# A decoder layer on one core: the gate of every early gate/up product through tanh, and a new order of calls

## The reference

```python
# x: (8,128,128), ctx: (8,128,128), mask: (8,128,128)
q, k, v = heads(x)                    # 16 heads, 64 wide
w   = softmax(causal(q @ k.T) / 8)
x1  = layernorm(x + concat(w @ v) @ w_o.T)
qc, kc, vc = x1 @ Wq.T + bq, ctx @ Wk.T + bk, ctx @ Wv.T + bv   # 16 heads, 8 wide
wc  = softmax(where(mask == 0, -1e9, qc @ kc.T / sqrt(8)))
x2  = layernorm(x1 + concat(wc @ vc) @ Wo.T + bo)
logits = x2 @ router_w.T              # 8 experts; top two, with a jitter threshold
dense_w = sparsemixer(logits)         # (tokens, 8), two entries per token
y = sum over e of dense_w[:, e] * ((silu(x2 @ w_gate[e].T) * (x2 @ w_up[e].T)) @ w_down[e].T)
out = layernorm(x2 + y)
```

## Time and profile before

| | |
|---|---|
| time, median of 3 | 233.08 us (233.04 to 233.16) |
| the profiled execution, its own time | 233.06 us |
| its span, first to last instruction | 231.0 us |
| TensorE busy | 225.9 us (98%) |
| VectorE busy | 192.1 us (83%) |
| ScalarE busy | 164.9 us (71%) |
| GpSimd busy | 102.0 us (44%) |
| granted TensorE clock | 1.00 throughout |

### The profile page before, as it was taken

One profiled execution on the slowest core, in us unless ns is written; L12 is line 12 of the kernel. 1 busy time (PEld: TensorE's weight loads), 2 busy tenths in 40 slices (PEclk: granted clock), 3 DMA queues, 4 the chain that ended last, 5 costly groups with the idle time before them and its releaser, 6 DMA issues.

```text
span 231.0 us, 6982 instructions
## 1 busy us (share of the span) xinstructions
PE 225.9 (98%) x2274; PEld 205.9 (89%) x2274; DVE 192.1 (83%) x954; ACT 164.9 (71%) x552; POOL 102.0 (44%) x162
## 2 busy tenths in 40 slices
PE   8999999999999999999999999999999999999992
PEld 8999888997978988978978988789999999999992
DVE  3897798997889889989899879989898565766984
ACT  3768988898999979999989999697476333333001
POOL 4387738796396568922978351231200000100112
PEclk9999999999999999999999999999999999999999
DMA  6998000000000000000002200000000000000000
GB/s 189 362 363 314 10 0 0 4 3 1 3 1 3 0 6 3 0 3 1 1 4 64 121 3 3 3 0 4 0 3 0 1 3 0 4 23 0 26 23 24
DMA packets 7011, 9.10 MB, mean 39 GB/s; under 512 B 1088, under 2 KB 5824, under 8 KB 6592
## 3 DMA queue, kind: packets, MB, share of 16 engines
q1 hardware_dynamic: 4320, 7.09, 8.7%
q10 hardware_dynamic: 2656, 1.57, 2.3%
HBM read 8.14 MB, written 0.52 MB: 37 GB/s over the span
## 4 chain that ended last, share of the span: by engine, by line
PE 96%; DVE 1%; issue 1%; POOL 1%; ACT 0%; POOLq 0%; ACTq 0%; DVEq 0%
PE bank L1545 13%; PE bank L1443 11%; PE bank L1445 10%; PE bank L1444 10%; PE bank L2043 9%; PE bank L1527 7%; PE bank L1554 7%; PE bank L1595 6%; PE bank L1563 4%; PE bank L1538 3%; PE bank L1611 2%; PE bank L1482 2%; PE bank L1483 2%; PE bank L1484 2%; PE bank L1570 2%; PE bank L2053 1%
## 5 line engine op out<-in xcount | busy, mean ns | idle before, releaser
L525 ACT ACTIVATE probs_s<-masked_s,nmax_s 128x128 f32<-128x128 f32 x128 | 49.8, 396 | 3.6 <-DVE nmax_s L839 2.1
L311 POOL TENSOR_TENSOR probs_s<-probs_s,rec_sum_s 128x512 f32<-128x512 f32 x32 | 33.1, 1040 | 35.0 <-DVE rec_sum_s L846 34.8
L586 ACT ACTIVATE silu<-bank 128x256 f32<-128x256 f32 x54 | 20.1, 384 | 30.3 <-PE bank L1445 28.4
L528 ACT ACTIVATE probs_c<-masked_c,nmax_c 128x128 f32<-128x128 f32 x128 | 40.3, 396 | 1.6 <-DVE nmax_c L839 1.4
L1443 PE MATMUL bank<-ctx_hi,gu_hi 128*128 128x256 f32 x128 | 38.7, 302 | 0.0
L1444 PE MATMUL bank<-ctx_lo,gu_hi 128*128 128x256 f32 x128 | 35.7, 279 | 0.0
L1445 PE MATMUL bank<-ctx_hi,gu_lo 128*128 128x256 f32 x128 | 35.7, 279 | 0.0
L839 DVE CUSTOM_DVE_ANT_0 masked_c<-bank,mask_add 128x128 f32<-128x128 f32 x128 | 29.0, 286 | 4.6 <-PE bank L1538 3.9
L839 DVE CUSTOM_DVE_ANT_0 masked_s<-bank,causal 128x128 f32<-128x128 f32 x128 | 29.2, 285 | 1.2 <-PE bank L1527 1.0
L503 POOL TENSOR_TENSOR mv<-mv,minus_half 128x1 f32<-128x1 f32 x7 | 3.8, 556 | 55.2 <-DVE mv L1388 55.2
L1443 PEld LDWEIGHTS bank<-ctx_hi,gu_hi 128*128 128x128 f32 x128 | 24.3, 190 | 0.7 <-DVE qk_a L969 0.3
(11 more groups left out here) (180 smaller groups left out, 591.4 us busy)
## 6 DMA issues: line engine op xcount, KB each, us to landing
raw<-in_gateT SPq DMA_DIRECT2D x1, 1024.0 KB, 8.2
raw<-in_upT SPq DMA_DIRECT2D x1, 1024.0 KB, 12.1
down_sb<-in_down SPq DMA_DIRECT2D x1, 1024.0 KB, 5.2
raw<-in_wvT SPq DMA_DIRECT2D x1, 512.0 KB, 5.6
ctxT_all<-in_ctxT SPq DMA_DIRECT2D x1, 512.0 KB, 6.9
masked_c<-in_mask ACTq DMA_DIRECT2D x1, 512.0 KB, 11.9
wo_sb<-in_woT SPq DMA_DIRECT2D x1, 512.0 KB, 6.1
x_tok<-in_x ACTq DMA_DIRECT2D x1, 512.0 KB, 11.2
```

The source lines that it names most:

```text
L311: pool.tensor_tensor(probs_s[:, g % 2], probs_s[:, g % 2], spread(rec_sum_s[:, 4 * g:4 * g + 4], 2, S), ALU.mult).then_inc(normed[g], 1)
L525: last = act.activation(probs_s[:, g % 2, i, :], masked_s[:, g % 2, i, :], ACT.Exp, scale=-1.0, bias=nmax_s[:, h:h + 1], accum_out=rsum_s[ ...
L528: last = act.activation(probs_c[:, g % 2, i, :], masked_c[:, g % 2, i, :], ACT.Exp, scale=-1.0, bias=nmax_c[:, h:h + 1])
L586: act.activation(silu[:, i % NS, :], g, ACT.Silu).then_inc(silued, 1)
```

## The change

`NTANH` goes from 10 to 32: products 10 to 31 take tanh on ScalarE and two instructions on VectorE. `gate` and `hidden` themselves are as before. `FILL_BANK` is another list; its last eight entries, the banks of products 24 to 31, are the same. All four lists of calls are written anew: the same calls with the same work, some in other places, many with other banks, and the written waits of TensorE to match. The diff, cut to the constants, to GpSimd around `own_k(6)` and `own_k(7)`, to ScalarE's and VectorE's late parts, and to TensorE's list from `gate_up(7)` on:

```diff
-    NTANH = 10
+    NTANH = 32
...
-        FILL_BANK = [OC, OC, X0, OS, OC, T1, Y0, X0, OC, X1, Y0, OS, X1, Y0, OS, T0,
-                     T1, Y0, X0, T1, X1, Y1, OC, T0, X0, Y0, OS, OC, X1, Y1, T0, T1]
+        FILL_BANK = [OC, X0, X0, Y0, OC, T1, Y0, X0, T0, Y1, X0, OC, T0, Y1, X0, OS,
+                     OC, Y0, X0, OS, Y1, X1, T0, T1, X0, Y0, OS, OC, X1, Y1, T0, T1]
...
 # GpSimd
+            padded_v(6)
+            normalise(0, 7)
+            root(var2_done, pow2_done, mv2, 3)
+            normalise(1, 7)
             own_k(6)
-            normalise(3, 6)
-            add_out_bias(5)
-            normalise(2, 6)
-            padded_v(5)
-            root(var2_done, pow2_done, mv2, 3)
-            own_k(7)
-            split_x2(1)
-            normalise(0, 7)
-            normalise(1, 7)
             root(var1_done, pow1_done, mv1, 6)
             normalise(2, 7)
             normalise(3, 7)
-            padded_v(6)
+            root(var2_done, pow2_done, mv2, 4)
             split_x2(2)
             add_out_bias(6)
-            root(var2_done, pow2_done, mv2, 4)
             root(var1_done, pow1_done, mv1, 7)
+            own_k(7)
             split_x2(3)
...
 # ScalarE
             gate(6)
             gate(7)
-            evac_turned("c", 2, 7, T0)
-            evac_turned("c", 3, 7, T1)
+            evac_turned("c", 2, 7, T1)
+            evac_turned("c", 3, 7, X1)
             gate(8)
             gate(9)
-            evac_oc(7, Y1)
+            evac_oc(7, OC)
             gate(10)
...
 # VectorE
             hidden(8)
             hidden(9)
-            divide_c(7, T0)
+            divide_c(7, Y0)
             hidden(10)
-            evac_ccatT(7, T0)
+            evac_ccatT(7, Y0)
             hidden(11)
+            evac_logits(5, OS)
+            residual2(7, X1)
+            hidden(12)
             evac_x2T(6, T1)
-            residual2(7, T0)
-            hidden(12)
-            evac_logits(5, X0)
             hidden(13)
             normalise_x2(7)
             hidden(14)
-            evac_x2T(7, X0)
+            evac_x2T(7, T1)
             evac_logits(6, X1)
             hidden(15)
-            evac_logits(7, OS)
+            evac_logits(7, T1)
+            hidden(16)
             rank_0()
-            hidden(16)
+            hidden(17)
             rank_1()
+            hidden(18)
             rank_2()
-            hidden(17)
+            hidden(19)
             rank_3()
-            hidden(18)
+            hidden(20)
             rank_4()
-            hidden(19)
+            hidden(21)
             rank_5()
-            hidden(20)
-            hidden(21)
             hidden(22)
             rank_6()
             hidden(23)
...
 # TensorE, around products 10 to 31 (the new list; unchanged ones between them left out)
+            pe.wait_ge(hid_done, 8)
             gate_up(10)
+            turn_oc(7, Y0)
+            gate_up(11)
+            turn_ccat(7, Y0)
+            gate_up(12)
+            route(5, OS)
+            project_out_c(7, X1)
+            gate_up(13)
+            gate_up(14)
             turn_x2(6, T1)
+            pe.wait_ge(logit_evac, 6)
             gate_up(15)
+            gate_up(16)
             route(6, X1)
+            turn_x2(7, T1)
             gate_up(17)
+            route(7, T1)
             gate_up(18)
-            pe.wait_ge(hid_done, 17)
+            pe.wait_ge(hid_done, 16)
             gate_up(19)
...
             pe.wait_ge(hid_done, 19)
             gate_up(24)
             gate_up(25)
+            pe.wait_ge(hid_done, 20)
             gate_up(26)
-            pe.wait_ge(hid_done, 23)
             gate_up(27)
+            pe.wait_ge(hid_done, 22)
             gate_up(28)
             gate_up(29)
+            pe.wait_ge(hid_done, 23)
+            gate_up(30)
             pe.wait_ge(hid_done, 24)
-            gate_up(30)
             gate_up(31)
```

More of the change, by code:

```diff
@@ L394, in _ @@
             split_x(1)
-            round_ctx(0)
             split_x(2)
@@ L399, in _ @@
             normalise(1, 0)
-            round_ctx(1)
-            split_cwk()
-            scale_cwq()
+            round_ctx(0)
+            key_bias()
             normalise(2, 0)
             normalise(3, 0)
-            key_bias()
+            split_cwk()
+            round_ctx(1)
+            scale_cwq()
+            padded_v(0)
+            split_gu(0)
             normalise(1, 1)
             normalise(0, 1)
+            own_k(0)
             normalise(3, 1)
@@ L410, in _ @@
             normalise(2, 1)
-            own_k(0)
-            split_gu(0)
             normalise(0, 2)
-            normalise(1, 2)
+            padded_v(1)
             add_out_bias(0)
             root(var1_done, pow1_done, mv1, 1)
+            normalise(1, 2)
+            add_out_bias(1)
             split_gu(1)
-            add_out_bias(1)
-            padded_v(0)
             own_k(1)
-            split_gu(2)
             normalise(2, 2)
@@ L424, in _ @@
             own_k(2)
-            padded_v(1)
+            root(var1_done, pow1_done, mv1, 2)
+            padded_v(2)
             normalise(0, 3)
-            root(var1_done, pow1_done, mv1, 2)
-            add_out_bias(2)
-            padded_v(2)
             normalise(1, 3)
             own_k(3)
-            split_gu(3)
             normalise(2, 3)
             normalise(3, 3)
-            split_gu(4)
-            normalise(0, 4)
-            root(var2_done, pow2_done, mv2, 0)
-            normalise(1, 4)
-            root(var1_done, pow1_done, mv1, 3)
-            padded_v(3)
-            add_out_bias(3)
-            split_gu(5)
-            normalise(2, 4)
+            split_gu(2)
+            own_k(4)
+            normalise(0, 4)
+            add_out_bias(2)
+            root(var1_done, pow1_done, mv1, 3)
+            normalise(1, 4)
+            root(var2_done, pow2_done, mv2, 0)
+            normalise(2, 4)
+            add_out_bias(3)
+            split_gu(3)
+            split_gu(4)
             normalise(3, 4)
-            split_gu(6)
-            split_gu(7)
-            own_k(4)
+            own_k(5)
             normalise(0, 5)
@@ L1147, in _ @@
+            group_max("s", 3, 3, Y0)
+            residual1(2, X0)
+            reciprocal_s(1, 3)
+            divide_c(0, T0)
+            reciprocal_s(0, 3)
+            group_max("s", 2, 3, Y1)
+            normalise_x1(2)
+            evac_v(3, 1, X0)
+            evac_x1T(2, OS)
+            evac_v(3, 0, T0)
+            evac_qk(3, 3, OC)
+            evac_qc(2, OS)
+            lower_qc(2, OS)
+            evac_ccatT(0, Y1)
             evac_turned("s", 1, 3, Y0)
+            group_max("c", 0, 2, OC)
@@ L1290, in _ @@
             group_max("c", 3, 7, OS)
[L1291 removed]
+            divide_c(6, X1)
+            evac_logits(4, T0)
+            evac_x2T(5, OC)
+            evac_ccatT(6, X1)
             hidden(5)
[L1293 to L1296 removed]
+            residual2(6, Y1)
             hidden(6)
@@ new lines, in _ @@
+            turn("s", 1, 1, Y0)
+            pe.wait_ge(v_evac[0], 2)
+            turn("s", 0, 1, X1)
+            pe.wait_ge(maxed["s"][2], 2)
+            project_out_s(0, OC)
+            project_v(2, 0, T0)
+            pe.wait_ge(kc_lower, 1)
+            next_qk(1, 0, OS)
+            pe.wait_ge(kc_lower, 2)
+            score_s(2, 0, X0, T1)
+            mix_s(1, 0, Y0)
+            turn("s", 2, 1, X1)
+            turn_x1(0, OC)
+            pe.wait_ge(qk_evac[0], 2)
+            turn("s", 3, 1, OS)
@@ L1919, in _ @@
+            turn("c", 0, 5, Y1)
+            turn("s", 1, 7, X1)
+            turn("c", 1, 5, T0)
+            pe.wait_ge(hid_done, 1)
+            route(1, OC)
+            pe.wait_ge(turned_evac["s"][0], 8)
+            turn_oc(4, OS)
+            gate_up(1)
+            pe.wait_ge(turned_evac["c"][0], 6)
+            turn_x1(6, Y1)
+            mix_s(7, 0, OC)
+            project_qc(6, T1)
+            turn("c", 2, 5, OS)
             pe.wait_ge(turned_evac["c"][1], 6)
-            turn("c", 2, 5, X0)
```

879 lines of the change are left out of this document (420 added, 459 removed).

## The result

The changed kernel took 242.54 us (median of 4 runs, 241.85 to 243.34) against 233.12 us before on the same chip: ratio 1.0403, 95% interval 1.038 to 1.0426, 9.4 us slower. The forecast was 239.0 us, with a range up to 241.5; the result lies outside. The profiled execution took 241.85 us with a span of 239.8 us, 8.8 us more than before.

What follows compares the result with a forecast made beforehand. TensorE's stream was taken to bound the kernel, with VectorE's second parts putting it behind. Profiled span 231.0 + 5.9 = 236.9 us, table loads and order adding nothing, + 2.06 = 239.0 us; range 236.2 to 241.5.

Steps and rivals of the forecast that it cites:

- The bound: TensorE's stream, busy 225.9 of 231.0 us, sets the time; VectorE is nearly as full from 148 to 177.5 us.
- The second parts, +5.9 us: Products 10 to 31 get a second VectorE instruction; TensorE's down_product(0, 3) then starts 5.9 us late.
- 9.9 - 0.8: VectorE's queue up to product 31: 22 x 0.45 = 9.9 us added, 0.8 us of it absorbed by pauses.
- The lower price, 0.11 us each: If a tanh product's first VectorE part cost only its pipelined 0.34 us: 2.4 us less, +3.5 in all.
- rival 1: Table loads decide and VectorE swallows the second parts: 232.8 us, or 230.5 with both loads on the path; chance 0.05.
- The table loads: On ScalarE one load is left, ahead of product 32; the saving is only the 0.26 us wait already in the 0.8.
- the cover that was named: The remaining load, near 184 us, has 2 us of cover before hidden(32); without it the load would cost 1.3.
- I take 0 for the whole order, between -3.1 and +1.5: The new order of calls in 0 to 157 us costs nothing, with bounds of -3.1 and +1.5 us.
- change nothing in this sum: The moved routing steps, the same ones in the same late stretch, add nothing to VectorE's queue.
- rival 4: TensorE's clock falls as it idles in 171 to 187 us: 4.6 us, 2 hidden behind VectorE, about 241.8; chance 0.07.
- Rival 2: The new order closes TensorE's holes, all 3.1 us gone and VectorE earlier by the same: 235.9 us; chance 0.10.
- rival 3: The new order opens holes through own_k(6) and its like: 0.8 to 1.5 us more, about 240.3; chance 0.08.

Runs made afterwards that it cites:

- e3: The changed kernel with products 27, 30 and 31 multiplied 3, 2 and 4 times over, so TensorE works through its holes; 241.69 us.
- e4: The changed kernel with GpSimd's own_k(7) moved from behind the last root of the first layernorm to behind normalise(3, 7); 241.18 us.
- t2: The changed kernel (32 tanh products) with own_k(7), split_gu(0) and spread_mask() moved, and the routing calls earlier; 240.17 us.
- t3: The changed kernel (32 tanh products) with own_k(7), split_gu(0) and spread_mask() moved, and TensorE's holes filled with repeated multiplications; 240.10 us.
- h4: The kernel before with 32 tanh products and product 26 multiplied four times over; 239.47 us.
- h3: The kernel before with 24 tanh products and product 26 multiplied four times over; 238.71 us.
- e1: The changed kernel with NTANH back at 10, the new order alone; 237.09 us, ratio 1.0161.
- t1: The new order with ten tanh products, own_k(7), split_gu(0) and spread_mask() moved, and the routing calls earlier; 234.46 us.
- h1: The new order with ten tanh products, own_k(7) and split_gu(0) put back, spread_mask() in a VectorE pause; 235.17 us.

## Why the prediction was wrong

**The bound.** Right: TensorE's stream sets the time, and the change put VectorE ahead of it in 170 to 187 us. Two readings on the way were wrong and changed no term: VectorE is busy 10.40 + 9.57 = 20.0 us of 148 to 170, not 19.3, which adds the weight loads' 9.73 of the first stretch to VectorE's 9.57 of the second; and in the old list bank T0 of product 23 goes to `gate_up(30)`, which started at 174.09, 1.4 us behind it, and not to `gate_up(31)` 2.1 us behind.

**The second parts, +5.9 us.** Right in each term. 0.79 us per product (182.12 to 182.90); VectorE 27.2 us from `divide_c(7)` to the operation behind product 31, against 18.2, +9.0 where 9.9 - 0.8 was forecast; no pause; the block of products 24 to 31 6.3 us. At full clock the distance is 31.15 to 31.23 us in four traces of the new order (e3, e4, t2, t3), 5.9 to 6.0 more than the 25.25 before, and 31.35 in h4, the old order. The lower price, 0.11 us each, and rival 1 are refuted. That 24 tanh products cost 5.4 us of distance at full clock (h3, 30.63 us) and 32 only 5.9 fits the same account.

**The table loads.** Right: one is left,

```profile
185.76 1.28 ACT L586 ACT_TABLE_LOAD   x1 [0.39 <-DVE qk_a L966]
```

in the cover that was named, 2.2 us ahead of `hidden(32)`. Rival 1's mechanism gave nothing.

**"I take 0 for the whole order, between -3.1 and +1.5": this step failed.** The order alone costs 3.7 us (3.3 to 4.2 by its interval), more than twice the upper bound; within the changed kernel, whose last stretch doesn't pay the 0.6, it is 1.5 us in the profiled run, and 2.2 by the medians, as what is left: 242.54 less 233.12, 5.95 and 1.3. The bound was built from one call, `own_k(6)`, as the worst place, and that place did little: the root there waited for VectorE's `mv`, to 131.89 us. Of `own_k(7)` I wrote "with little to spare" and gave it no price. It cost 0.7 us in the new order and 1.35 in the old one, and not by being late: I had priced GpSimd's calls only by when they end, and not by what they hold while they run. The rows for that were in hand: two 1.04 us operations put directly behind the operation that releases a VectorE one. Two other places showed. The mask call ahead of `reciprocal_s(3, 0)` costs 0.8 to 1.1 us where the mask lands late, by the traces of e1 and e3; moving it brought the medians nothing clear. The routing calls behind two more products cost 0.4 us, with ten products only. I had priced both as free: of the routing I wrote that it would "change nothing in this sum", and the mask call I never named.

**The clock, rival 4 at 0.07.** It happened in all four runs of the changed kernel (mean clock 0.983 to 0.993), with the mechanism as described and a smaller price: in the profiled run 3.41 us at half clock, of which 1.3 reach the end (32.52 against 31.2), where 2.6 was forecast. That the lower level doubles a step is right by the changed kernel's own rows: `gate_up`'s matmuls start 0.21 us apart from 184.19 us on and 0.12 apart from 187.64 on. The 20 matmuls of the earlier trace rows could not show it: they are as slow as that, but the profile has the granted clock at 1.00 over them. The chance was too low. I had the idle third of 171 to 187 us in my own account of the changed kernel, and took the forecast's clock from a stretch in which TensorE never stopped.

Together, for the profiled run: 239.0 forecast, +1.3 for the clock, +1.5 for the order, 241.8, and it took 241.85. The median lies 0.7 us above that run; the mask's landing can do as much, but the other runs have no trace. Both errors have one sign, and each was a rival with a chance of its own; the range of 236.2 to 241.5 held either one alone, not the two together. Rival 2 (the new order closes holes) is refuted by the order alone; rival 3 was right in kind, at other places, and at 1.5 to 2.2 us where it had 0.8 to 1.5.

**What stays open.** t1 is still 1.3 us above the kernel before. In h1, which has the same start, TensorE shows no wait between 17.9 and 40.2 us and yet needs 22.3 us for the same calls that took 21.7. Which neighbours of calls make that I did not separate. h1's six runs still differ by 1 us with the mask out of the way; why, no trace shows, and `project_cv(0)` alone starts up to 0.8 us apart in the traces. Nor was the new order tried with its GpSimd calls moved from beside the other `normalise_x1` calls: the first of them took 1.21 us in the changed kernel, at 34.43, against 0.34 before, and two more took 0.76 and 0.94. Why the clock falls in one run of a kernel and not in the next stays open too.

## What to carry to other kernels

Where VectorE and GpSimd both work in SBUF, price a moved GpSimd operation by what VectorE has to do while it runs, and not only by its own start and end; the worst place is directly behind the small operation that VectorE waits for. If an added load puts a second engine ahead of TensorE, add the clock: TensorE's holes can cost again behind them, and more instructions put into the hole can make the kernel faster. Compare runs with the fall with runs that have it. And an order made anew is not free because it holds the same calls: each call that stands behind other work than before is a term of the sum. A call that waits for a transfer costs in some executions and not in others, so one trace can put down its price too high or miss it.

## What the runs showed of the hardware

- A VectorE operation of 128x128 floats from SBUF to SBUF took 0.35 us alone and 1.05 beside a GpSimd operation of 1.03 us that had begun 0.06 us ahead, and ended 0.08 us behind it. VectorE operations that read a bank (0.24 and 0.29 us) showed no such hold beside the second of the two GpSimd operations.
- Eighteen more matmul instructions in an idle 2.4 us made the kernel with 24 tanh products 1.1 us faster, 239.84 to 238.71, by keeping the granted clock at 1.00.
- The same program had the clock fall in some runs only: routing early with 32 products in one of five, 241.30 us against 239.83 to 240.37; the changed kernel with `own_k(7)` early in three of five, 241.18 to 241.62 us against 240.42 and 240.60.
- The 512 KB transfer of the mask landed 7.1 to 13.6 us after its issue in 17 traces.
